# Twelve chunks on GpSimd in projecting blocks, with other feeds, block ends and token phases, in an fp32 attention layer kernel

## The chip, the cores and the metric

The kernel runs on one core of a Trainium2 chip. The metric is the device time of one execution in microseconds (us). A kernel is one program for the core's engines: TensorE (PE; its weight loads are PEld), VectorE (DVE), ScalarE (ACT), GpSimd (POOL) and SyncE (SP), which here issues every DMA. The engines run their own instruction lists in order and meet only at semaphores. Times from the trace are counted from the start of the span.

## The reference, cut to what matters

Four sequences (batches) of 2048 tokens and 512 features pass through one attention layer with 16 heads of 32 features, and a small feed-forward layer.

```python
q, k, v = x @ Wq.T + bq, x @ Wk.T + bk, x @ Wv.T + bv       # split into 16 heads of 32
scores  = einsum('bqhd,bkhd->bhqk', q, k) / sqrt(32) + bias  # bias: -inf on 3 key columns
attn    = softmax(scores, axis=-1)
ctx     = einsum('bhqk,bkhd->bqhd', attn, v)
y       = layernorm(x + ctx @ Wo.T + bo) * gamma + beta
x1      = layernorm(x + y)
xq      = quantize_4bit(x1 @ Hadamard)                       # scale from the row's largest value
out     = layernorm(x1 + einsum(xq, ternary(W)))
```

## The kernel before, in words

**Blocks.** A block is one group of 4 heads (there are 4 groups, `NG`) and 512 queries (4 per sequence, `NQB`), so a batch has 16 blocks (`NBLK`), and the run 64, numbered n; i is the block's place in its batch. Block i serves group i // 4. Its 2048 keys are cut into 16 chunks of 128 (`NKC`), and the chunks go in 8 pairs, p = 0 to 7.

**What one block does.** For each chunk and head PE multiplies keys by queries (`score`, L522) into one of three PSUM banks `ps_s`; ACT takes the exponential into `prob` (L740); PE multiplies the probabilities by the values into `ps_o` (`context`, L545). `prob` has slots for only 6 chunks (`NPB`), so the exponential of chunk c waits until PE and POOL have read chunk c - 6. The softmax needs each row's maximum one block ahead: for the next block's queries PE computes the scores once more in another layout, 64 units of 128 queries by 512 keys (`unit`, L507), into three banks `ps_m`, and DVE takes the maximum of each (L882). In `feed` every score of this block is followed by a unit for the next block.

**The softmax's sums.** They are column sums of `prob` over all chunks. Eleven chunks are added up by POOL into `acc` (L1074, ten additions of 128x2048 elements), and PE sums the other five, chunks 9 and 12 to 15 (`PE_SUMS`), with ones as weights (`column_sums`, L527, 4 matmuls a chunk). PE then adds `acc` in the same way; that releases the reciprocal on DVE (`zinv`, L894), and this releases POOL's `normalise` of the finished context (L1058, L1061), which goes before POOL's additions of the next block.

**The order at a block's end.** After feed 7 PE does context pair 6 with the sums of chunks 12 and 13, the transposition of the maxima (L514), the sums of chunks 14 and 15, the sum of `acc`, and context pair 7. The transposed maxima go by ACT (L730, `mrow`) and two DMAs (L331) into two rows of the query operand `qst`; the next block's first score waits for them (`q_cur`). `qst` has two buffers. Once the last score of block n is done, SP copies the queries of block n + 2 into n's buffer with three DMAs (`queries`, L283: high part, high part, low part; semaphore `q_stk`), and then issues the two of the maxima. The first unit of block n + 1 works on those queries.

**Projections.** During block n PE projects the queries of block n + 2 after feed 0 (L494), ACT writes out their high part and DVE their low part. In the places i = 4 to 15 (in the last batch 4 to 11), called projecting, it also projects a quarter of the next group's keys (L462, after context pair 1) and values (L468, after feed 4). There are 12 x 3 + 8 = 44 such blocks. All these use the bank `ps_z`, which later takes the column sums.

**The token phase.** After block 15 come 21 steps over the batch's 16 tiles of 128 tokens: output projection (L598) plus the residual (L601), layer norms, Hadamard transform, quantization and the feed-forward product, spread over all engines. Its tiles lie in `prob`, `hi` and `lo`; the output weights lie in the unused half of `vst`. `load_parameters` (L351) loads three quarters of the output weights and the row parameters during block 15; the fourth quarter and the first two tiles come in `load_first_tiles` (L362), after the DMAs of queries and maxima. In the last four steps of the first three batches the keys and values of the next batch's second group are projected too (`keys_quarter`, L285), each with a 1 MB load for a later projection. At the end all engines wait in `batch_done` (L100) until the last output tiles have been stored. Then a loop branches back; the last batch is written out after the loop.

## Time and profile before

| what | value |
|---|---|
| median of 3 runs (lowest to highest) | 4933.66 us (4932.66 to 4935.23) |
| the profiled execution's own time | 4934.81 us |
| its span | 4933.0 us |
| mean granted TensorE clock | 0.98 |
| busy: PE, PEld, DVE, ACT, POOL | 96%, 49%, 67%, 52%, 69% |
| longest groups, us busy | L1074 2638.0 + 290.6; L882 2495.1; L740 2087.7; L507 1796.1; L522 1738.7; L545 1000.0 |

The profile counts an engine as busy while an instruction of it runs. Matmuls overlap, so a busy PE is not one at its peak. A bracket behind a row of the timeline tells how long the engine had been idle and who ended that; "issue" means that the profile shows nothing waited for. The profiled execution's time is 1.8 us above its span and 1.15 us above the median of the runs.

### The profile page before, as it was taken

To read this page: it belongs to the slowest core of one execution; us is meant where nothing else is said; L and a number is where in the kernel's file an instruction comes from. 1 tells how busy PE (TensorE), PEld (TensorE's weight loads), DVE (VectorE), ACT (ScalarE), POOL (GpSimd) and SP (SyncE) were. 2 spreads that over 40 slices of the span, in tenths; PEclk is the share of its full clock that TensorE was granted. 3 is DMA by queue.
4 is the path that set the end of the run, shared out by engine and by line. 5 is a ranking of instruction groups with operands and counts; after the bars stand their busy time and mean duration, and the time that the engine had idled before them with its cause. 6 is when DMAs were issued, how large, how long until landed. Compare 5 with 4: busy or idle time off the path is not lost.

```text
span 4933.0 us, 84699 instructions
## 1 busy us (share of the span) xinstructions
PE 4724.2 (96%) x24536; PEld 2427.2 (49%) x24536; DVE 3299.1 (67%) x5886; ACT 2543.4 (52%) x4891; POOL 3420.8 (69%) x1167
## 2 busy tenths in 40 slices
PE   7999999999899999999979999999998999999997
PEld 4445455554444555455444455555545445455434
DVE  3776666666677666666667766666676766666737
ACT  1455555554455555555445555555545555555645
POOL 1687766776477777777738877777764887777885
PEclk8899999999999999999989999999999999999998
DMA  8113233333411333233441133323343123323112
GB/s 204 31 40 65 63 70 69 63 67 99 125 38 42 67 68 68 61 69 69 105 117 40 40 69 63 67 67 69 61 118 97 39 54 69 63 64 74 29 50 73
DMA packets 247838, 346.34 MB, mean 70 GB/s; under 512 B 16721, under 2 KB 102481, under 8 KB 247378
## 3 DMA queue, kind: packets, MB, share of 16 engines
q1 hardware_dynamic: 247378, 340.73, 30.0%
q8 instruction: 225, 3.69, 0.3%
q14 instruction: 235, 1.93, 0.1%
HBM read 205.33 MB, written 33.55 MB: 48 GB/s over the span
## 4 chain that ended last, share of the span: by engine, by line
PE 83%; issue 6%; POOL 4%; DMA 3%; DVE 2%; SPq 1%; ACT 1%; DVEq 0%; POOLq 0%; ACTq 0%
PE ps_m L507 23%; PE ps_s L522 21%; PE ps_o L545 17%; PE ps_z L527 6%; PE ps_z L494 4%; PE ps_z L468 3%; PE ps_z L462 3%; DMA qst<-mrow 1%; DVE umax L882 1%; POOL prob L1100 1%; POOL prob L1104 1%; PE ps_s L468 1%; PE ps_s L462 1%; POOL prob L1089 1%; POOL prob L1083 1%
## 5 line engine op out<-in xcount | busy, mean ns | idle before, releaser
L882 DVE TENSOR_REDUCE umax<-ps_m 128x1 f32<-128x512 f32 x4096 | 2495.1, 682 | 1020.0 <-PE ps_m L507 1019.7
L1074 POOL TENSOR_TENSOR acc<-acc,prob 128x2048 f32<-128x2048 f32 x576 | 2638.0, 4580 | 134.0 <-ACT prob L740 84.9
L740 ACT ACTIVATE prob<-ps_s 128x512 f32<-128x512 f32 x4096 | 2087.7, 619 | 704.8 <-PE ps_s L522 703.3
L507 PE MATMUL ps_m<-kst,qst 97*128 97x512 f32 x4096 | 1796.1, 441 | 18.3 <-DVE umax L882 15.7
L522 PE MATMUL ps_s<-qst,kst 99*128 99x512 f32 x4096 | 1738.7, 425 | 75.0 <-issue 34.5
L522 PEld LDWEIGHTS ps_s<-qst,kst 99*128 99x128 f32 x4096 | 776.1, 190 | 633.9 <-issue 380.3
L507 PEld LDWEIGHTS ps_m<-kst,qst 97*128 97x128 f32 x4096 | 780.9, 191 | 550.1 <-DVE umax L882 427.6
L545 PE MATMUL ps_o<-prob,vst 128*32 128x512 f32 x8192 | 1000.0, 600 | 0.0
L1058 POOL TENSOR_TENSOR obuf<-obuf,zinv 128x512 f32<-128x512 f32 x64 | 82.0, 1281 | 785.5 <-DVE zinv L894 785.5
L1074 POOL TENSOR_TENSOR acc<-prob 128x2048 f32<-128x2048 f32 x64 | 290.6, 4541 | 359.1 <-ACT prob L740 359.1
L894 DVE RECIPROCAL zinv<-ps_z 128x512 f32<-128x512 f32 x64 | 214.9, 3358 | 345.5 <-PE ps_z L527 345.5
L545 PEld LDWEIGHTS ps_o<-prob,vst 128*32 128x32 f32 x8192 | 220.8, 109 | 456.4 <-issue 316.8
L527 PE MATMUL ps_z<-prob,ones 128*32 128x512 f32 x2560 | 322.8, 595 | 0.0
L598 PE MATMUL ps_s<-vst,hi 128*128 128x512 f32 x512 | 239.1, 611 | 21.3 <-DMA hi<-ctxT_dram 21.3
L494 PE MATMUL ps_z<-xq,wq 128*128 128x512 f32 x496 | 224.1, 594 | 0.0
L765 ACT ACTIVATE obuf<-ps_o 128x512 f32<-128x512 f32 x64 | 38.3, 598 | 275.0 <-PE ps_o L545 275.0
L468 PEld LDWEIGHTS ps_z<-wkv,xk 128*128 128x128 f32 x1408 | 160.5, 192 | 36.9 <-issue 36.9
L468 PE MATMUL ps_z<-wkv,xk 128*128 128x128 f32 x1408 | 168.9, 278 | 0.0
L462 PE MATMUL ps_z<-xk,wkv 128*128 128x512 f32 x352 | 162.8, 605 | 0.0
L1082 POOL TENSOR_TENSOR prob<-prob 128x256 f32<-128x256 f32 x64 | 46.7, 730 | 164.7 <-ACT prob L778 164.7
L598 PEld LDWEIGHTS ps_s<-vst,hi 128*128 128x128 f32 x512 | 96.4, 197 | 127.7 <-issue 102.8
L527 PEld LDWEIGHTS ps_z<-prob,ones 128*32 128x32 f32 x2560 | 76.7, 110 | 161.4 <-issue 134.6
(115 smaller groups left out, 2461.5 us busy)
## 6 DMA issues: line engine op xcount, KB each, us to landing
xk<-in_xT_dram SPq DMA_DIRECT2D x66, 1024.0 KB, 5.6
xq<-in_xT_dram SPq DMA_DIRECT2D x65, 1024.0 KB, 5.6
kst<-hi SPq DMA_DIRECT2D x128, 256.0 KB, 6.8
qst<-hi SPq DMA_DIRECT2D x128, 256.0 KB, 5.6
wq<-in_wT_dram SPq DMA_DIRECT2D x65, 256.0 KB, 5.8
kst<-lo SPq DMA_DIRECT2D x64, 256.0 KB, 5.7
qst<-lo SPq DMA_DIRECT2D x64, 256.0 KB, 6.8
ctxT_dram<-obuf SPq DMA_DIRECT2D x64, 256.0 KB, 2.4
```

The source lines that it names most:

```text
L462: mm = nc.tensor.matmul(bank, wkv[:, 0, c], xk[:, t % 2, c], start=c == 0, stop=c == IC - 1)
L468: mm = nc.tensor.matmul(bank[:, u * P:(u + 1) * P], xk[:, t % 2, c, u * P:(u + 1) * P], wkv[:, 1, c], start=c == 0, stop=c == IC - 1)
L494: mm = nc.tensor.matmul(bank, wq[:, c], xq[:, c], start=c == 0, stop=c == IC - 1)
L507: nc.tensor.matmul(ps_m[:, u % NMB, :], qst[k % 2][0:RSTACK, h, qt * P:(qt + 1) * P], kst[k // NQB % 2][0:RSTACK, h, kb * QB:(kb + 1) * QB ...
L522: nc.tensor.matmul(ps_s[:, (i * HG * NKC + HG * c + h) % NSB, :], kst[i // NQB % 2][0:RALL, h, c * P:(c + 1) * P], qst[i % 2][0:RALL, h, : ...
L527: mm = nc.tensor.matmul(ps_z[HD * h:HD * h + HD, :], ones[:, 0:HD], src[:, h, :], start=first, stop=last)
L545: mm = nc.tensor.matmul(ps_o[HD * h:HD * h + HD, :], vst[:, i // NQB % 2, c, HD * h:HD * h + HD], prob[:, c % NPB, h, :], start=c == 0, st ...
L598: nc.tensor.matmul(ps_wo[t % 3], tC[t % 2][:, h * P:(h + 1) * P], wo_sb[:, h, :], start=h == 0, stop=False)
L740: nc.scalar.activation(prob[:, c % NPB, h, :], ps_s[:, (i * HG * NKC + HG * c + h) % NSB, :], ACT.Exp, scale=SCALE).then_inc(ex, 1)
L882: nc.vector.tensor_reduce(umax[:, m, kb:kb + 1], ps_m[:, u % NMB, :], AX.X, ALU.max).then_inc(mred, 1)
L894: nc.vector.reciprocal(zinv[:], ps_z[:]).then_inc(zrec, 1)
L1074: nc.gpsimd.tensor_tensor(acc[:], a, prob[:, c % NPB], ALU.add).then_inc(padd, 1)
```

## The change

It does several things, which the diff below shows at their core:

- `pe_sums(i)`: in places i = 4 to 15 of every batch PE sums chunks 12 to 15 only, and POOL adds up twelve chunks in eleven additions. In places 0 to 3 the division stays. `added(n, i)` counts POOL's additions, which now differ by place.
- `feed` issues the unit ahead of the score.
- The block's end on PE: feed 7, the sums of chunks 12 to 15, the transposition of the maxima, the sum of `acc`, context pair 6, context pair 7.
- SP issues the two high parts of the queries, then the maxima as one DMA (`q_cur` counts 16 instead of 32), then the queries' low part.
- ACT writes out projected queries, keys and values one pair of chunks later.
- Token phase, start: the last quarter of the output weights goes to a slot of `prob` that is free after chunk 11; the first token tile goes into `hi[1]` and `lo[1]` and is loaded within `load_parameters`; the second one after the stacks of the queries have landed.
- Token phase, end: `batch_done` is gone. PE waits for its own phase's DVE results, and ACT, at chunk 3 of the next batch's first block, for the stores. The two 1 MB loads for the next group are issued after the last step (`next_stage`) and no longer in the third and fourth `keys_quarter`; this holds for the beginning of the run too.

```diff
-PE_SUMS = [9, 12, 13, 14, 15]
-POOL_SUMS = [c for c in range(NKC) if c not in PE_SUMS]
-NADD = len(POOL_SUMS) - 1
+LATE_SUMS = NKC - 4
+W_CHUNK = 11
+def pe_sums(i):
+    return [12, 13, 14, 15] if i >= NQB else [9, 12, 13, 14, 15]
+def pool_sums(i):
+    return [c for c in range(NKC) if c not in pe_sums(i)]
+def additions(i):
+    return len(pool_sums(i)) - 1
...
-        tC = [hi[:, t, :].bitcast(F32) for t in range(2)]
-        tX = [lo[:, t, :].bitcast(F32) for t in range(2)]
+        tC = [hi[:, 1 - t, :].bitcast(F32) for t in range(2)]
+        tX = [lo[:, 1 - t, :].bitcast(F32) for t in range(2)]
+        tW = [wo_sb[:, g, :] for g in range(IC - 1)] + [rows[:, 23, :]]
...
             def keys_quarter(stage, b, s, t):
-                wait_alone(sp, vproj, stage * NQB + t + 1, passed)
                 if t < 2:
+                    wait_alone(sp, vproj, stage * NQB + t + 1, passed)
                     load_x(xk[:, t], batch_of(b, s * NQB), t + 2).then_inc(xk_ld[t], 16)
-                else:
-                    load_x(xk[:, t - 2], batch_of(b, (s + 1) * NQB), t - 2).then_inc(xk_ld[t - 2], 16)
...
+            def next_stage(stage, b, s):
+                for t in range(2):
+                    wait_alone(sp, vproj, stage * NQB + t + 3, passed)
+                    load_x(xk[:, t], batch_of(b, (s + 1) * NQB), t).then_inc(xk_ld[t], 16)
                 next_weights(s)
...
-                stack(qst[k % 2], (hi[:, 0], hi[:, 0], lo[:, 0]), q_stk)
+                stack(qst[k % 2], (hi[:, 0], hi[:, 0]), q_stk)
+            def low_queries(f, k):
+                sp.wait_ge(q_lo, f + 1)
+                sp.dma_start(qst[k % 2][2 * HD:3 * HD].bitcast(F32), lo[:, 0].bitcast(F32)).then_inc(q_stk, 16)
...
-                for r in range(2):
-                    row = qst[k % 2][RM0 + r:RM0 + r + 1].rearrange("p h x -> p (h x)")
-                    sp.dma_start(row.bitcast(F32), mrow[HG * NQB * r:HG * NQB * (r + 1), :].bitcast(F32)).then_inc(q_cur, 16)
+                both = qst[k % 2][RM0:RM0 + 2].rearrange("p h (q x) -> p (h q) x", x=P)
+                sp.dma_start(both.bitcast(F32), mrow[:].bitcast(F32)).then_inc(q_cur, 16)
...
-            def load_parameters(n):
+            def load_parameters(n, last):
                 for g in range(IC - 1):
                     load_projection(n, g)
+                wait_alone(sp, k_stk[1], ((n >> 4) * NG + NG + (0 if last else 1)) * (2 * NSTK), passed)
+                wait_alone(sp, cst, (n >> 4) * (NBLK * 16) + NBLK * 16, passed)
+                load_rows((n >> 4) & (NB - 1), 0)
+                load_context((n >> 4) & (NB - 1), 0)
...
+            def load_last_projection(n):
+                wait_alone(sp, pv, n * NKC + NKC + W_CHUNK + 1, passed)
+                wait_alone(sp, padd, added(n, NBLK - 1) + (addition_of(NBLK - 1, W_CHUNK) + 1), passed)
+                sp.dma_start(tW[IC - 1], woT[(IC - 1) * P:, :]).then_inc(c_par, 16)
+            def load_second_tile(b, last):
+                wait_alone(sp, k_stk[0], (b * NG + NG + (0 if last else 1)) * (2 * NSTK), passed)
+                wait_alone(sp, q_stk, (b * NBLK + NBLK + (0 if last else 2)) * NSTK, passed)
+                load_rows(b, 1)
+                load_context(b, 1)
...
                         if not (last and i >= NBLK - 2):
-                            queries(n + 2, (n >> 4) & (NB - 1), i + 2)
+                            queries(n + 2, i + 2)
                         if not (last and i == NBLK - 1):
                             maxima(n + 1, i + 1)
+                        if not (last and i >= NBLK - 2):
+                            low_queries(n + 2, i + 2)
...
                     for h in range(HG):
-                        score(n, i, c, h, head=i == 0 and c == 0)
                         if not (last and i == NBLK - 1):
                             unit(HG * c + h, n + 1, i + 1, (n >> 2) + 1 if i % NQB == NQB - 1 else None)
+                        score(n, i, c, h, head=i == 0 and c == 0)
...
-                    context(n, i, p - 1)
+                    if p < NP - 1:
+                        context(n, i, p - 1)
...
+                for c in pe_sums(i):
+                    if c >= LATE_SUMS:
+                        chunk_sums(n, i, c)
                 if not (last and i == NBLK - 1):
                     maxima_to_rows(n + 1)
-                for c in PE_SUMS:
-                    if c >= NKC - 2:
-                        chunk_sums(n, i, c)
-                pe.wait_ge(padd, n * NADD + 2 * NADD)
+                pe.wait_ge(padd, added(n, i) + additions(i))
                 column_sums(acc, False, True).then_inc(zdone, 1)
+                context(n, i, NP - 2)
                 context(n, i, NP - 1)
...
+                wait_alone(pe, c_y, b * NT + NT, passed)
+                wait_alone(pe, c_fo, b * NT + NT, passed)
...
-                batch_done(pe, c_st, b, passed)
...
             def attend(n, i, stage, last):
                 for c in range(NKC):
+                    if i == 0 and c == 14 // HG:
+                        for k in range(NST):
+                            act.wait_ge(c_st[k], (n >> 4) * (16 * stored_by(k, NT)) + 16)
...
-                    if p == 0 and not (last and i >= NBLK - 2):
+                    if p == 1 and not (last and i >= NBLK - 2):
...
-                    if projects(i, last) and p == KEY_PAIR:
+                    if projects(i, last) and p == KEY_PAIR + 1:
...
-                    if projects(i, last) and p == VALUE_PAIR:
+                    if projects(i, last) and p == VALUE_PAIR + 1:
```

## Rows read from the trace of the kernel before

**Rows 1.** The page: busy time, and the chain that ended last, by engine.

```profile
PE 4724.2 (96%) x24536; PEld 2427.2 (49%) x24536; DVE 3299.1 (67%) x5886; ACT 2543.4 (52%) x4891; POOL 3420.8 (69%) x1167
PE 83%; issue 6%; POOL 4%; DMA 3%; DVE 2%; SPq 1%; ACT 1%; DVEq 0%; POOLq 0%; ACTq 0%
```

**Rows 2.** Stretches: busy us (count) by engine; PE clock, DMA share, GB/s.

```profile
383.50:1112.30 728.80, 720.47 (x3884) 370.63 (x3884) 486.70 (x782) 384.15 (x759) 524.80 (x132) 1.00 0.31 66
4546.50:4775.60 229.10, 224.96 (x1171) 100.27 (x1171) 133.19 (x211) 136.46 (x266) 191.09 (x48) 0.97 0.13 31
```

**Rows 3.** Timeline of DVE within a projecting block: start us, us, what, [idle before].

```profile
408.39 4.88 DVE L882 TENSOR_REDUCE umax<-ps_m 128x1 f32<-128x512 f32 x8 [4.76 <-PE ps_m L507]
...
414.59 4.88 DVE L882 TENSOR_REDUCE umax<-ps_m 128x1 f32<-128x512 f32 x8 [0.66 <-PE ps_m L507]
424.36 4.88 DVE L882 TENSOR_REDUCE umax<-ps_m 128x1 f32<-128x512 f32 x8 [4.89 <-PE ps_m L507]
431.42 0.69 DVE L882 TENSOR_REDUCE umax<-ps_m 128x1 f32<-128x512 f32 x1 [2.18 <-PE ps_m L507]
```

**Rows 4.** Timeline around the ends of two successive blocks, n = 5 and 6.

```profile
510.87 0.28 PE L514 MATMUL ps_m<-ident,msplit 128*32 128x128 f32 x1
...
511.48 1.22 SPq L331 DMA_DIRECT2D qst<-mrow  x2
...
514.00 3.36 DVE L894 RECIPROCAL zinv<-ps_z 128x512 f32<-128x512 f32 x1 [4.67 <-PE ps_z L527]
...
516.77 0.49 PE L522 MATMUL ps_s<-qst,kst 99*128 99x512 f32 x1 [1.19 <-DMA qst<-mrow]
...
577.34 0.28 PE L514 MATMUL ps_m<-ident,msplit 128*32 128x128 f32 x1
...
582.11 0.50 PE L522 MATMUL ps_s<-qst,kst 99*128 99x512 f32 x1
```

**Rows 5.** DMA issues: size, us to landing; first a stack alone at its issue, then medians of 64.

```profile
qst<-hi SPq DMA_DIRECT2D x1, 256.0 KB, 4.2
...
qst<-lo SPq DMA_DIRECT2D x64, 256.0 KB, 6.8
ctxT_dram<-obuf SPq DMA_DIRECT2D x64, 256.0 KB, 2.4
```

**Rows 6.** Timeline of POOL in block 6 and blocks 62, 63, with PE's block starts.

```profile
521.51 4.54 POOL L1074 TENSOR_TENSOR acc<-prob 128x2048 f32<-128x2048 f32 x1 [1.80 <-ACT prob L740]
527.44 41.84 POOL L1074 TENSOR_TENSOR acc<-acc,prob 128x2048 f32<-128x2048 f32 x9 [1.39 <-ACT prob L740]
...
4665.06 0.50 PE L522 MATMUL ps_s<-qst,kst 99*128 99x512 f32 x1 [1.25 <-DMA qst<-mrow]
...
4674.57 42.41 POOL L1074 TENSOR_TENSOR acc<-acc,prob 128x2048 f32<-128x2048 f32 x9
...
4720.41 0.96 PE L522 MATMUL ps_s<-qst,kst 99*128 99x512 f32 x3
```

**Rows 7.** Timeline at the start of the first token phase.

```profile
1173.57 0.28 PE L514 MATMUL ps_m<-ident,msplit 128*32 128x128 f32 x1
...
1183.73 6.51 PE L598 MATMUL ps_s<-vst,hi 128*128 128x512 f32 x8 [5.45 <-DMA hi<-ctxT_dram]
...
1190.93 3.60 PE L598 MATMUL ps_s<-vst,hi 128*128 128x512 f32 x8
```

**Rows 8.** From the end of the first token phase to block 16.

```profile
1337.38 3.73 PE L468 MATMUL ps_s<-wkv,xk 128*128 128x128 f32 x32
...
1343.13 0.81 ACT L783 ACTIVATE prob<-prob,lnv 128x512 f32<-128x512 f32 x1 [1.20 <-DVE lnv L936]
1344.92 0.36 SPq L376 DMA_DIRECT2D out_dram<-prob  x1
...
1357.75 0.79 PE L522 MATMUL ps_s<-qst,kst 99*128 99x512 f32 x1 [16.63 <-issue]
...
L694 PEldq COMPARE_BRANCH  x3: 77/3332/5025, 1354.1 to 3777.7; - x3
```

More of the change, by code:

```diff
@@ L42 @@
 KEY_PAIR, VALUE_PAIR = 2, 4
-POOL_SUMS = [c for c in range(NKC) if c not in PE_SUMS]
-NADD = len(POOL_SUMS) - 1
-ADD_OF = {c: max(i - 1, 0) for i, c in enumerate(POOL_SUMS)}
+LATE_SUMS = NKC - 4
 NT = L // P
@@ L52, with addition_of, added @@
 PAR_SLOT = 4
+W_CHUNK = 11
 KEY_STEP = NT - 1
+def pe_sums(i):
[4 more added lines that the diff above has]
+    return len(pool_sums(i)) - 1
+def addition_of(i, c):
+    return max(pool_sums(i).index(c) - 1, 0)
+def added(n, i):
+    return (n >> 4) * sum(additions(k) for k in range(NBLK)) + (additions(NBLK - 1) + sum(additions(k) for k in range(i)))
 def former_chunk(c):
@@ L97, in stored_by @@
     return len([i for i in range(t) if i % NST == k])
-def batch_done(eng, c_st, b, passed):
-    for k in range(NST):
-        wait_alone(eng, c_st[k], b * (16 * stored_by(k, NT)) + 16 * stored_by(k, NT), passed)
 def build(nc, x, xT, wT, bqkv, woT, w_ffn, band, gamma, beta, bo, had, out):
@@ L360, in load_parameters @@
                 sp.dma_start(bob, bo.partition_broadcast(P)).then_inc(c_par, 16)
-            def load_first_tiles(b, n, last):
-                load_projection(n, IC - 1)
-                for t in range(2):
-                    wait_alone(sp, k_stk[t], (b * NG + NG + (0 if last else 1)) * (2 * NSTK), passed)
+            def load_last_projection(n):
[4 more added lines that the diff above has]
+                wait_alone(sp, k_stk[0], (b * NG + NG + (0 if last else 1)) * (2 * NSTK), passed)
                 wait_alone(sp, q_stk, (b * NBLK + NBLK + (0 if last else 2)) * NSTK, passed)
-                wait_alone(sp, cst, b * (NBLK * 16) + NBLK * 16, passed)
-                for t in range(2):
-                    load_rows(b, t)
-                    load_context(b, t)
+                load_rows(b, 1)
+                load_context(b, 1)
             def tokens(b, last):
@@ L405, in _ @@
             sp.sem_inc(cst, 16)
+            for k in range(NST):
+                sp.sem_inc(c_st[k], 16)
             keys(0, 0, 0)
@@ L412, in _ @@
             sp.wait_ge(mask_ld, 2 * HG * 16)
-            queries(0, 0, 0)
+            queries(0, 0)
+            low_queries(0, 0)
             next_queries(0, 0)
             keys(1, 0, 1)
-            queries(1, 0, 1)
+            queries(1, 1)
+            low_queries(1, 1)
             next_queries(0, 1)
@@ L546, in context @@
                                               prob[:, c % NPB, h, :], start=c == 0, stop=c == NKC - 1)
-                    if c in PE_SUMS and p < NP - 1:
+                    if c in pe_sums(i) and c < LATE_SUMS:
                         mm = chunk_sums(n, i, c)
@@ L597, in tokens @@
                             for h in range(NG):
-                                nc.tensor.matmul(ps_wo[t % 3], tC[t % 2][:, h * P:(h + 1) * P], wo_sb[:, h, :],
+                                nc.tensor.matmul(ps_wo[t % 3], tC[t % 2][:, h * P:(h + 1) * P], tW[h],
                                                  start=h == 0, stop=False)
@@ L737, in exponential @@
                     act.wait_ge(pv, n * NKC + k + 1 + (0 if before else NKC))
-                    if k in POOL_SUMS:
-                        act.wait_ge(padd, n * NADD + ADD_OF[k] + 1 + (0 if before else NADD))
+                    j = (i - 1) % NBLK if before else i
+                    if k in pool_sums(j):
+                        act.wait_ge(padd, added(n, i) - (additions(j) if before else 0) + (addition_of(j, k) + 1))
                 nc.scalar.activation(prob[:, c % NPB, h, :], ps_s[:, (i * HG * NKC + HG * c + h) % NSB, :],
@@ L744, in attend @@
                 for c in range(NKC):
+                    if i == 0 and c == 14 // HG:
+                        for k in range(NST):
+                            act.wait_ge(c_st[k], (n >> 4) * (16 * stored_by(k, NT)) + 16)
                     for h in range(HG):
@@ L1061, in normalise, with attend @@
                 nc.gpsimd.tensor_scalar(obuf[:], obuf[:], 1.0, bias[:, g:g + 1], ALU.mult, ALU.add).then_inc(cbias, 1)
-            def attend(n):
-                for k in range(NADD):
-                    c = POOL_SUMS[k + 1]
+            def attend(n, i):
+                for k in range(additions(i)):
+                    c = pool_sums(i)[k + 1]
                     pool.wait_ge(ex, n * (HG * NKC) + HG * c + HG)
@@ L1069, in attend @@
                         pool.wait_ge(zdone, n + 1)
[L1070 removed]
+                        a = prob[:, pool_sums(i)[0] % NPB]
                     else:
[L1072 removed]
+                        pool.wait_ge(padd, added(n, i) + k)
                         a = acc[:]
@@ L1129, in _ @@
             pool.wait_ge(mask_ok, 2)
-            pool.sem_inc(padd, NADD)
+            pool.sem_inc(padd, additions(NBLK - 1))
             pool.sem_inc(cbias, 1)
```

43 lines of the change are left out of this document (20 added, 23 removed).

## The prediction

> **What bounds the kernel now.** I read the page first: PE is busy for 96% of the span, its chain is 83% of the time, POOL 4%, DMA 3%, and "issue" 6% [rows 1]. So what PE does counts, and the gaps between its pieces. The stretch of eleven projecting blocks confirms it: 720.47 of 728.8 us busy, at the full granted clock, a block every 728.8 / 11 = 66.25 us [rows 2]. Within a block the timeline of DVE shows two facts. Its maxima come in bursts of 8, one a pair of chunks, and DVE idles 0.66 us or more before each burst, waiting for PE: PE sets the pace, though inside a burst DVE does. And a pair without column sums takes 414.59 - 408.39 = 6.20 us, one with the sums of a chunk 431.42 - 424.36 = 7.06 us, both with one context pair between the bursts [rows 3]. Four sum matmuls thus cost 0.86 us of the path. The ends of blocks and of batches come last; there PE waits for DMAs and for a branch [rows 4, 7, 8].
>
> **The change, part by part.**
>
> *1. A chunk from PE to POOL.* In 44 projecting blocks the four matmuls of chunk 9 go: 44 x 0.86 = 38 us less. POOL pays an addition of 41.84 / 9 = 4.65 us [rows 6]. Does it keep up? In block 6 its last addition ends at 527.44 + 41.84 = 569.28, which is 52.5 us after the block's start at 516.77 [rows 4]; with one more, at 57.2. PE will want `acc` right after the transposition, at 577.34 - 516.77 = 60.6 us, less 0.86: 59.7. So 2.5 us of cover are left. If that goes, each us past it costs 44. The exponential of chunk 15, now behind the addition of chunk 9, is covered too: that addition ends two before the last, 48 us into the block, and chunk 15 belongs to the last feed, just ahead of the 59.7.
>
> *2. The last batch's places 12 to 15 have no projection, and still get eleven additions.* Before, blocks 60 to 63 took 4775.6 - 4546.5 = 229.1 us together [rows 2]. In block 62 POOL's additions end at 4674.57 + 42.41 = 4716.98, 51.9 us after the start, and the block is 55.3 us long [rows 6]: 3.4 us lie behind the last addition. With 4.65 us more, and context pair 6 (1.7 us, 8 matmuls of 0.213) now behind the sum of `acc`, POOL becomes the bound: 51.9 + 4.7 + 3.4 + 1.7 = 61.7, where it was 55.3. The other three get the same bound: 4 x 61.7 = 247, 18 us more than the 229.1.
>
> *3. The block's end.* Before, one of two things delays the next block: the maxima's second DMA (1.19 us before block 6), or the reciprocal, which keeps DVE from the first units until 3.36 us after it starts [rows 4]. Block 6 began behind its wait, with DVE free, and took 582.11 - 516.77 = 65.34; the mean is 66.25, so the two cost 0.9 us a block. After: behind the transposition stand as many matmuls as before (4 of `acc` and 16 of context instead of 12 sums and 8), so PE is ready at the same 582.11 - 577.34 = 4.8 us after it. The reciprocal starts 8 matmuls, 1.7 us, earlier and is gone by then. The maxima's single DMA is 0.6 us earlier. But the first instruction is now a unit, and it waits for the queries' low part, whose DMA stands behind the maxima's on SP: issued 511.48 - 510.87 + 0.61 = 1.2 us after the transposition. This DMA was never seen alone. From below, it lands like the 256 KB context store, in 2.4 us: no wait. From above, like today's low part, third in its row, 6.8 us. A stack of the same shape with nothing ahead takes 4.2 [rows 5], and the two high parts are nearly drained by then, so I take 4.2: landing at 5.4, a wait of about 0.7 at each start. Against 0.9 that is 0.2 less a block, 10 us in all. The Trainium skill, "DMA: Bandwidth & Descriptors", section "Anatomy of one DMA", puts a DMA at about 2.0 us plus its bytes at 436 GB/s; that would be 2.6 us here and no wait, and the sum 38 us lower. The 2.4 us store agrees with it, the stack of 4.2 doesn't.
>
> *4. Unit before score, and ACT's later write-outs.* DVE gets its burst's first unit one matmul earlier and the feed ends one score later: nothing. A write-out now follows 8 exponentials; DVE wants the result after its own burst, which ends at about the same time, and the bank isn't used before. Nothing; from above 0.3 us a block (a write-out that delays a burst), 18 us.
>
> *5. The start of a token phase.* Before, PE waits 5.45 us for the first context tile and runs it at the low clock, 6.51 us instead of 3.60. The first matmul stands 1183.73 - 1173.57 = 10.2 us behind the transposition [rows 7]; after, at 4.8, at the full clock. That gains up to 5.4 + 2.9 us. The second tile is later than PE could take it: its load waits for the stacks of the queries, which queue behind more parameters, landing about 9 us and the tile 12 us behind the transposition. I take 5.5 us for three batches and 7 for the last, which has no such stacks: 23.5 us less. The bounds are nothing and 4 x 8.3 = 33 us.
>
> *6. The end of a token phase.* PE's last matmul ends at 1341.1; the last output store is issued at 1344.92, its landing lets the branch begin at 1354.1, this takes 3.33 us, and block 16 starts at 1357.75: 16.63 us idle [rows 8]. After, PE can branch at 1342, but ACT ends its last tile at 1343.94 and DVE at about the same time, and both branch too. Block 16 then starts near 1346, its exponentials near 1350. I take 9.5 us for each of the two branches and 9.6 for the third change of batch, which has none, and 1.5 for the time at the low clock: 30 us less. The Trainium skill, "Runtime: NRT & Kernel Launch", section "Instruction fetch mechanics", says that a taken branch out of the fetched pages waits for a DMA. The row agrees (3.3 and 5.0 us against 0.08 for the one not taken); beside key stacks it could be longer. The stores are waited for at chunk 3, some 14 us into the block: covered; without that cover, up to 7 us a batch.
>
> *7. The beginning.* The 1 MB loads move behind the key stacks, while the DMA engines are busy throughout: the same bytes ahead of the same weights. Nothing, within 5 us either way.
>
> Sum: -38 + 18 - 10 + 0 - 23.5 - 30 = -83.5. From the profiled execution's 4934.8 that is 4851.3, and 4850 against the median, which is 1.15 lower.
>
> **Rivals.**
>
> *No wait for the low part* (chance 0.14). The DMA lands within 3.6 us of its issue. 57 block starts x 0.7 = 40 us less: 4810. For it: the store of 2.4. Against: the stack of 4.2, which has the same shape and nothing ahead.
>
> *The low part becomes the wait at every block's start* (0.06). If it takes the 6.8 us of today, it lands 8.0 us behind the transposition, PE idles 3.2 us where I have 0.7, and 57 x 2.5 = 143 us come on top: 4993, slower than before. It decides from a landing about 5.7 us after issue, since 83.5 / 57 = 1.5 us a block uses the gain up. For it: the only row of a low part. Against: that row has two stacks right ahead of it.
>
> *POOL bounds the projecting blocks* (0.06). If its chain ends 1.5 us past the 2.5 us of cover, 66 us come back: 4916. For it: its chain fills 57 of 65 us. Against: its additions hardly vary, 4.65 us in block 6 and 42.41 / 9 = 4.71 in block 62.
>
> *The token phases give little* (0.12). The first steps are held by the second tile, the branch by DMA traffic: 30 of 53.5 us stay away: 4880.
>
> *The change does not do what it says* (0.03): chunk 9 stays on the path, as ACT waits for POOL at chunk 15, and the rest cancels: about 4930.
>
> **How the numbers follow.** My forecast has 0.59, with a range of its own of 4835 to 4868. The range goes from 4805 to 4890: it takes in the case without a wait and weak token phases, and leaves out the low part at 6.8, the POOL bound and the change without effect. No change means within 0.2%, 10 us, which is about what a measurement of this kernel can tell. Faster 0.92, the same 0.03, slower 0.05.
>
> **What would show it.** L527 has 48 x 4 = 192 fewer matmuls, and POOL 48 more additions. Projecting blocks come every 65.2 us. The first unit of a block shows an idle time of about 0.7 us ended by the DMA into `qst` from `lo`; over 2 us means the second rival, none the first. The reciprocal ends before the block's first maximum. Blocks 60 to 63 wait for POOL and take 247 us. PE's idle time at the first token phase's start is under 1 us, at its end near 5 us. Wrong would be: a POOL wait before `acc` in projecting blocks, waits of ACT for POOL, or a token phase of the same length.

## The result, and the profile after

The changed kernel takes 4856.6 us in the median of its runs (4853.13 to 4858.9) against 4934.44 us for the kernel before (4932.66 to 4937.3) on the same chip: a ratio of 0.9841, with a 95% interval of 0.983 to 0.9853. The prediction was 4850 us, with a range of 4805 to 4890. The profiled execution took 4853.13 us; its span is 4851.3 us, where the span before was 4933.0, so 81.7 us have to be accounted for; the sum of the prediction was 83.5.

The page of the changed kernel, busy time and the chain that ended last, then two of its groups (busy us, mean ns of one, idle time before them):

```profile
PE 4667.5 (96%) x24152; PEld 2379.4 (49%) x24152; DVE 3320.0 (68%) x5886; ACT 2586.8 (53%) x4891; POOL 3641.8 (75%) x1215
PE 79%; POOL 7%; DMA 6%; issue 4%; DVE 2%; ACT 1%; SPq 1%; POOLq 0%; ACTq 0%; DVEq 0%
L1115 POOL TENSOR_TENSOR acc<-acc,prob 128x2048 f32<-128x2048 f32 x624 | 2857.6, 4580 | 117.8 <-ACT prob L780 64.8
L543 PE MATMUL ps_m<-kst,qst 97*128 97x512 f32 x4096 | 1885.5, 463 | 57.4 <-DMA qst<-lo 36.9
```

Against [rows 1], PE has 384 records fewer (192 matmuls, each of two records), and POOL has 48 instructions more: the chunk moved as announced. POOL's part of the chain rose from 4% to 7%, the DMAs' from 3% to 6%, and "issue" fell from 6% to 4%. The new DMA share has a name in the last line: PE waits 36.9 us for the queries' low part, at 57 starts of blocks, and this DMA alone is 5% of the chain.

The two stretches of [rows 2], now places 4 to 14 of the first batch and blocks 60 to 63:

```profile
381.30:1096.80 715.50, 708.18 (x3796) 362.31 (x3796) 489.60 (x781) 391.16 (x760) 575.42 (x144) 1.00 0.30 67
4446.40:4699.80 253.40, 230.49 (x1141) 100.03 (x1142) 133.81 (x210) 139.03 (x265) 208.83 (x52) 0.93 0.12 33
```

A projecting block now takes 715.5 / 11 = 65.05 us where it took 66.25. The last four blocks take 253.4 us where they took 229.1, at a lower granted clock (0.93 where it was 0.97).

The timeline of all engines around the end of block 6, with the DMA issue of the low part in a view of the DMAs of that microsecond (median us to landing), answers to [rows 4, 5]:

```profile
570.95 0.28 PE L550 MATMUL ps_m<-ident,msplit 128*32 128x128 f32 x1
571.16 1.07 PE L563 MATMUL ps_z<-acc,ones 128*32 128x512 f32 x8
...
571.56 0.69 SPq L355 DMA_DIRECT2D qst<-mrow  x1
572.04 3.62 PE L581 MATMUL ps_o<-prob,vst 128*32 128x512 f32 x32
572.30 0.57 SPq L345 DMA_DIRECT2D qst<-lo  x1
572.36 3.36 DVE L936 RECIPROCAL zinv<-ps_z 128x512 f32<-128x512 f32 x1 [3.19 <-PE ps_z L563]
...
576.47 0.50 PE L543 MATMUL ps_m<-kst,qst 97*128 97x512 f32 x1 [0.81 <-DMA qst<-lo]
...
577.00 0.69 DVE L924 TENSOR_REDUCE umax<-ps_m 128x1 f32<-128x512 f32 x1 [1.28 <-PE ps_m L543]
```

```profile
qst<-lo SPq DMA_DIRECT2D x1, 256.0 KB, 4.0
```

The low part is issued 1.35 us after the transposition and lands 4.0 us later; PE is ready 576.47 - 0.81 - 570.95 = 4.7 us after the transposition and idles 0.81 us. The reciprocal ends at 575.72, before DVE's first maximum.

POOL's ten later additions in block 6, from its timeline, answer to [rows 6]:

```profile
521.98 46.50 POOL L1115 TENSOR_TENSOR acc<-acc,prob 128x2048 f32<-128x2048 f32 x10 [1.03 <-ACT prob L780]
```

They end at 568.48, and the sum of `acc` runs at 571.16 without a wait: 2.7 us of cover are left. In block 60, which has no projection, that cover is gone. PE there, and the stretch from the end of its wait, with the granted clock (third figure from the end):

```profile
4499.34 0.28 PE L550 MATMUL ps_m<-ident,msplit 128*32 128x128 f32 x1
4503.97 1.93 PE L563 MATMUL ps_z<-acc,ones 128*32 128x512 f32 x8 [4.34 <-POOL acc L1115]
4505.67 5.33 PE L581 MATMUL ps_o<-prob,vst 128*32 128x512 f32 x32
4510.94 0.50 PE L543 MATMUL ps_m<-kst,qst 97*128 97x512 f32 x1
```

```profile
4503.90:4511.00 7.10, 7.03 (x41) 1.64 (x41) 3.36 (x1) 0.00 (x0) 0.01 (x1) 0.63 0.00 0
```

PE idles 4.34 us for the last addition, and then the granted clock is 0.63 in the mean, near the lower of its two levels (1.2 GHz is 0.5): the sum and the two context pairs take 1.93 and 5.33 us where the end of block 6 had 1.07 and 3.62.

The start of the first token phase, PE and DVE, answers to [rows 7]:

```profile
1156.44 0.28 PE L550 MATMUL ps_m<-ident,msplit 128*32 128x128 f32 x1
...
1161.09 2.84 PE L636 MATMUL ps_s<-vst,hi 128*128 128x512 f32 x6
...
1165.47 1.12 PE L639 MATMUL ps_s<-prob,ident 128*128 128x512 f32 x2 [0.68 <-POOL prob L1141]
...
1166.63 0.70 DVE L1014 BATCH_NORM_STATS2 stats<-ps_s 128x6 f32<-128x512 f32 x1 [5.41 <-PE ps_s L639]
...
1167.91 2.84 PE L636 MATMUL ps_s<-vst,hi 128*128 128x512 f32 x6 [1.32 <-DMA hi<-ctxT_dram]
```

The output projection follows the last context matmul with no gap, 4.65 us after the transposition, at the full clock (granted clock 1.00, where the same matmuls before had 0.56).

The end of that token phase, the branch at the loop's end (count, shortest, median and longest in ns) and the DMA share beside it (second figure from the end of its line), answer to [rows 8]:

```profile
1313.25 3.73 PE L504 MATMUL ps_s<-wkv,xk 128*128 128x128 f32 x32
...
1319.00 0.81 ACT L826 ACTIVATE prob<-prob,lnv 128x512 f32<-128x512 f32 x1 [1.20 <-DVE lnv L978]
1320.05 0.34 SPq L405 DMA_DIRECT2D out_dram<-prob  x1
...
1325.25 0.79 PE L543 MATMUL ps_m<-kst,qst 97*128 97x512 f32 x1 [8.26 <-issue]
```

```profile
L733 PEldq COMPARE_BRANCH  x3: 77/7009/7032, 1317.9 to 3686.2; - x3
```

```profile
1317.90:1324.90 7.00, 0.00 (x0) 0.00 (x0) 0.89 (x6) 0.81 (x1) 0.00 (x0) 0.73 1.04 202
```

PE branches 0.9 us after its last matmul ends, without waiting for the store, which is issued only afterwards. But the branch takes 7.0 us where it took 3.33, beside DMA engines that are busy throughout. The idle time is 8.26 us, where it was 16.63.

**Where the 81.7 us lie.** The starts of the blocks in the two traces give this account:

| part | before, us | after, us | difference, us |
| --- | --- | --- | --- |
| 44 projecting blocks | 66.23 each | 65.03 each | -52.8 |
| 12 blocks in places 1 to 3 | 59.12 each | 58.85 each | -3.2 |
| blocks 60 to 63 | 229.1 | 253.4 | +24.3 |
| three token phases | 179.3, 179.3, 173.6 | 163.4, 163.5, 157.1 | -48.1 |
| last token phase | 157.4 | 151.5 | -5.9 |
| blocks 16, 32, 48 | 184.3 | 189.9 | +5.6 |
| up to the end of block 0 | 206.3 | 204.7 | -1.6 |

The lengths of blocks are means over the whole run, so that of a projecting block is 0.02 us below the one of the first batch. A token phase here runs from the start of the batch's last block to that of the next batch's first, less the length of a projecting block. The sum is -81.7. In the last row two things hide each other: block 0 starts 4.8 us earlier (140.4 instead of 145.2) and is 3.2 us longer (64.4 instead of 61.2).

### The profile page after: what moved, and what is told of

Read it like the earlier page. It is cut to its first block, busy times and chain, and to the rows that moved or that the text cites. A ratio compares the mean times of both kernels' runs of the same rounds, so it can differ in the third digit from the quotient of the medians.

```text
span 4851.3 us, 83916 instructions
## 1 busy us (share of the span) xinstructions
PE 4667.5 (96%) x24152; PEld 2379.4 (49%) x24152; DVE 3320.0 (68%) x5886; ACT 2586.8 (53%) x4891; POOL 3641.8 (75%) x1215
## 4 chain that ended last, share of the span: by engine, by line
PE 79%; POOL 7%; DMA 6%; issue 4%; DVE 2%; ACT 1%; SPq 1%; POOLq 0%; ACTq 0%; DVEq 0%
PE ps_m L543 25%; PE ps_s L558 19%; PE ps_o L581 15%; PE ps_z L563 5%; DMA qst<-lo 5%; PE ps_z L530 4%; PE ps_z L504 3%; PE ps_z L498 3%; POOL acc L1115 3%; POOL prob L1141 1%; POOL prob L1145 1%; PE ps_s L504 1%; POOL prob L1130 1%; POOL prob L1124 1%; PE ps_s L498 1%
## 5 line engine op out<-in xcount | busy, mean ns | idle before, releaser
L1115 POOL TENSOR_TENSOR acc<-acc,prob 128x2048 f32<-128x2048 f32 x624 | 2857.6, 4580 | 117.8 <-ACT prob L780 64.8
L780 ACT ACTIVATE prob<-ps_s 128x512 f32<-128x512 f32 x4096 | 2131.3, 610 | 1293.3 <-PE ps_s L558 1231.2
L543 PE MATMUL ps_m<-kst,qst 97*128 97x512 f32 x4096 | 1885.5, 463 | 57.4 <-DMA qst<-lo 36.9
L558 PE MATMUL ps_s<-qst,kst 99*128 99x512 f32 x4096 | 1635.8, 400 | 12.0 <-ACT prob L780 9.8
L581 PE MATMUL ps_o<-prob,vst 128*32 128x512 f32 x8192 | 976.8, 600 | 0.0
L563 PE MATMUL ps_z<-prob,ones 128*32 128x512 f32 x2176 | 253.0, 602 | 0.0
L636 PE MATMUL ps_s<-vst,hi 128*128 128x512 f32 x384 | 176.1, 594 | 3.8 <-DMA hi<-ctxT_dram 3.8
L504 PEld LDWEIGHTS ps_z<-wkv,xk 128*128 128x128 f32 x1408 | 160.5, 192 | 36.9 <-issue 36.9
L769 ACT ACTIVATE mrow<-ps_m 32x128 fp32r<-32x128 f32 x64 | 17.0, 266 | 245.1 <-PE ps_m L550 245.1
L530 PEld LDWEIGHTS ps_z<-xq,wq 128*128 128x128 f32 x496 | 96.2, 194 | 97.6 <-issue 91.6
```

Source lines behind the costliest of these rows:

```text
L504: mm = nc.tensor.matmul(bank[:, u * P:(u + 1) * P], xk[:, t % 2, c, u * P:(u + 1) * P], wkv[:, 1, c], start=c == 0, stop=c == IC - 1)
L530: mm = nc.tensor.matmul(bank, wq[:, c], xq[:, c], start=c == 0, stop=c == IC - 1)
L543: nc.tensor.matmul(ps_m[:, u % NMB, :], qst[k % 2][0:RSTACK, h, qt * P:(qt + 1) * P], kst[k // NQB % 2][0:RSTACK, h, kb * QB:(kb + 1) * QB ...
L558: nc.tensor.matmul(ps_s[:, (i * HG * NKC + HG * c + h) % NSB, :], kst[i // NQB % 2][0:RALL, h, c * P:(c + 1) * P], qst[i % 2][0:RALL, h, : ...
L563: mm = nc.tensor.matmul(ps_z[HD * h:HD * h + HD, :], ones[:, 0:HD], src[:, h, :], start=first, stop=last)
L581: mm = nc.tensor.matmul(ps_o[HD * h:HD * h + HD, :], vst[:, i // NQB % 2, c, HD * h:HD * h + HD], prob[:, c % NPB, h, :], start=c == 0, st ...
```

## The experiments

Every kernel below is the changed kernel (4856.6 us) with the edit shown; times are medians. A ratio is to the kernel before, run beside it on the same chip (medians of 4934.4 to 4936.2 us).

**Chunk 9 back on TensorE.**

```diff
-    return [12, 13, 14, 15] if i >= NQB else [9, 12, 13, 14, 15]
+    return [9, 12, 13, 14, 15]
```

> The changed kernel with PE summing chunk 9 again in every place, so ten additions everywhere. If the sum matmuls are on the path, projecting blocks rise from 65.0 to 65.9 us (44 x 0.86 = 38 us more), and blocks 60 to 63 fall from 253 to about 228 us (25 less, as POOL no longer holds PE): about 4870 us. Rival, that POOL's slower pace already held the projecting blocks or that the gain came from the new order alone: projecting blocks stay at 65.0 and the kernel gets faster, about 4832 us.

Measured: 4943.23 us, ratio 1.0021 to before (1.0011 to 1.003). Neither expectation holds: it is 87 us slower than the changed kernel, where step 1 less step 2 would be 20. Blocks 60 to 63 take 231.4 us, as they should, but projecting blocks take 67.4 us. PE's waits (us in total, times, longest) name a line that has no wait in the changed kernel:

```profile
PE ps_o L581 <- issue: 54.3, 44, 1.4
```

44 is the number of projecting blocks. It stands ahead of context pair 4, with which chunk 9's sums begin. These sums write to the bank `ps_z`, in which the projected values still lie, so `attend` waits there for `v_cp`, ACT's write-out of them; and the change has moved this write-out one pair later. The next run tells whether that is it.

**Chunk 9 on TensorE, and the values written out as early as before.** The edit above, and in ACT's `attend`:

```diff
-                    if projects(i, last) and p == VALUE_PAIR + 1:
+                    if projects(i, last) and p == VALUE_PAIR:
```

> The changed kernel with chunk 9 on TensorE in all blocks, and with the write-out of the values by ScalarE after pair 4's exponentials again, as before the change, instead of after pair 5's. Theory (the later write-out is free only because chunk 9 has left TensorE: its sums need the bank ps_z that the values lie in, so TensorE waits for ScalarE): projecting blocks come down from 67.2 us to some 65.8 us, and the time from 4943.2 to some 4870 to 4880 us. Rival (the 67.2 us come from the block end or from the adds of GpSimd): they stay at 67.2 us and the time at 4943 us.

Measured: 4872.46 us, ratio 0.987 (0.9853 to 0.9886); projecting blocks 65.91 us. The theory holds: one pair of delay costs 70.8 us when chunk 9's sums stand behind it. This kernel is also the changed one less the chunk's move, and so it prices steps 1 and 2: projecting blocks 65.91 - 65.03 = 0.88 us longer (44 x 0.88 = 38.7), the last four 253.4 - 231.4 = 22.0 shorter, 16.7 together against 15.9 measured.

**All write-outs early, chunk 9 on GpSimd.**

```diff
-                    if p == 1 and not (last and i >= NBLK - 2):
+                    if p == 0 and not (last and i >= NBLK - 2):
...
-                    if projects(i, last) and p == KEY_PAIR + 1:
+                    if projects(i, last) and p == KEY_PAIR:
...
-                    if projects(i, last) and p == VALUE_PAIR + 1:
+                    if projects(i, last) and p == VALUE_PAIR:
```

> The changed kernel with all three write-outs of ScalarE (queries, keys, values) one pair earlier, where they were before the change. If the prediction's fourth step is right (their place costs and gives nothing while chunk 9 is on GpSimd), the projecting blocks stay at 65.05 us and the time at 4856.6 us within 5 us. Rival (a later write-out keeps ScalarE from making TensorE wait for its exponentials): each of 64 blocks is 0.2 to 0.4 us longer, 4870 to 4882 us.

Measured: 4856.97 us, projecting blocks 65.05 us. The place of the write-outs costs and gives nothing once chunk 9 has left PE.

**Eleven additions only where a block projects.** `pe_sums` returns the old list for places 12 to 15 of the last batch (`LAST` is set for it), and the counts of additions follow.

```diff
-    return [12, 13, 14, 15] if i >= NQB else [9, 12, 13, 14, 15]
+    full = i == -1 or NQB <= i < (NBLK - NQB if LAST[0] else NBLK)
+    return [12, 13, 14, 15] if full else [9, 12, 13, 14, 15]
```

> The changed kernel with the eleven additions in the 44 projecting blocks alone; blocks 60 to 63 go back to ten additions and chunk 9 on PE. If POOL is what holds these four, they fall from 253 us to the 228 or so that their PE work and boundaries need, and the half-clock stretches in them go: about 4832 us. Rival, that the context pair behind the sum of acc is what made them longer: they fall by half of that at most, 4845 us.

Measured: 4834.72 us, ratio 0.98 (0.9784 to 0.9816), 21.9 us under the changed kernel. PE's waits for `acc` fall from 14.2 us to 3.5 in the whole run, and the four blocks take 232.8 us together. So the eleventh addition is what held them; the 3.7 us over the 229.1 of before remain, and what they come from was not tried.

**The low part ahead of the maxima on SP.**

```diff
-                        if not (last and i == NBLK - 1):
-                            maxima(n + 1, i + 1)
                         if not (last and i >= NBLK - 2):
                             low_queries(n + 2, i + 2)
+                        if not (last and i == NBLK - 1):
+                            maxima(n + 1, i + 1)
```

> The changed kernel with the queries' low part issued right behind the two high parts, ahead of the maxima. If the low part's DMA is the wait at a block's start (0.8 us at 57 starts), it goes: up to 0.6 us a block, 34 us, is gained, 4825 us, and blocks start at 4.7 us behind the transposition. Rival, that the maxima's DMA then becomes the wait, since it queues behind three stacks as it did before the change (landed 4.3 to 5.8 us behind the transposition): the first score instead of the first unit waits, and the gain is between 0 and 15 us, 4845 us.

Measured: 4822.94 us, ratio 0.9777 (0.9761 to 0.9793), 33.7 us under the changed kernel. The same block boundary in this kernel:

```profile
566.63 0.60 SPq L345 DMA_DIRECT2D qst<-lo  x1
...
568.77 0.28 PE L550 MATMUL ps_m<-ident,msplit 128*32 128x128 f32 x1
...
569.38 0.69 SPq L355 DMA_DIRECT2D qst<-mrow  x1
...
573.66 0.50 PE L543 MATMUL ps_m<-kst,qst 97*128 97x512 f32 x1 [0.18 <-DMA qst<-lo]
```

The low part is now issued right behind the high parts, 2.1 us ahead of the transposition; it takes 7 us from there, with two stacks right ahead of it (one alone takes 4.2 us [rows 5]), and the wait falls from 0.81 to 0.18 us. Projecting blocks take 64.42 us.

**Each score ahead of its unit.** The two calls in `feed` change places.

```diff
+                        score(n, i, c, h, head=i == 0 and c == 0)
                         if not (last and i == NBLK - 1):
                             unit(HG * c + h, n + 1, i + 1, (n >> 2) + 1 if i % NQB == NQB - 1 else None)
-                        score(n, i, c, h, head=i == 0 and c == 0)
```

> The changed kernel with each score ahead of its unit of maxima again, as before the change. If the prediction's fourth step is right (the order of the two costs and gives nothing within a block), the projecting blocks stay at 65.05 us; at a block's boundary the first score then stands ahead of the unit that waits 0.7 to 0.8 us for the low part, but it waits for the maxima's rows itself, so that little or nothing is gained: 4850 to 4862 us. Rival (the unit ahead of the score is what feeds VectorE early enough): 0.3 us or more for each of 64 blocks, 4875 us or more.

Measured: 4843.23 us, ratio 0.9814 (0.9799 to 0.9829): 13.3 us under the changed kernel, below both expectations.

```profile
569.20 0.28 PE L550 MATMUL ps_m<-ident,msplit 128*32 128x128 f32 x1
...
573.84 0.50 PE L558 MATMUL ps_s<-qst,kst 99*128 99x512 f32 x1
...
574.56 0.59 ACT L780 ACTIVATE prob<-ps_s 128x512 f32<-128x512 f32 x1
574.61 0.50 PE L543 MATMUL ps_m<-kst,qst 97*128 97x512 f32 x1 [0.27 <-DMA qst<-lo]
```

The first score works on the other buffer of queries and does not wait for the low part: it runs 4.64 us after the transposition, in the time that the unit spends waiting, and ACT's exponentials start earlier. The maxima follow the transposition almost as before (5.94 us behind it, where the changed kernel has 6.05). What this saves shows at the block's end. The last unit, the late sums behind it, and what stands between them, first in the changed kernel, then in this one:

```profile
566.71 0.19 PEld L543 LDWEIGHTS ps_m<-kst,qst 97*128 97x128 f32 x1 [0.30 <-DVE umax L924]
567.04 0.40 PE L558 MATMUL ps_s<-qst,kst 99*128 99x512 f32 x1
...
567.38 3.64 PE L563 MATMUL ps_z<-prob,ones 128*32 128x512 f32 x32
```

```profile
565.19 0.19 PEld L543 LDWEIGHTS ps_m<-kst,qst 97*128 97x128 f32 x1 [0.30 <-DVE umax L924]
...
565.63 3.64 PE L563 MATMUL ps_z<-prob,ones 128*32 128x512 f32 x32
```

In both kernels the last unit waits for DVE to free a bank. Unit first, one more score stands behind it, and the sums start 0.67 us after the unit; score first, they start after 0.44. From DVE's last maximum to the next transposition it is 2.26 us instead of 2.49. So score first moves one score of each block from the end, where it delays the next transposition, into the wait at the start. Projecting blocks take 64.79 us, 0.24 less; block 0 is 3.0 us shorter, which is nearly all of the 3.2 us that the change had made it longer by.

**The first token tile loaded late again.**

```diff
-                load_rows((n >> 4) & (NB - 1), 0)
-                load_context((n >> 4) & (NB - 1), 0)
...
-                load_rows(b, 1)
-                load_context(b, 1)
+                for t in range(2):
+                    load_rows(b, t)
+                    load_context(b, t)
```

> The changed kernel with the first token tile's rows and context loaded where they were loaded before the change, behind the tail stores of the last block instead of ahead of them. If the prediction's fifth step is right, the start of the token phase loses most of what it gained: 5 to 7 us in each of 4 batches, 4877 to 4885 us. Rival (the gain there came from the wait for the last block's stores that left the other engines): under 2 us a batch, some 4860 us.

Measured: 4870.82 us, ratio 0.9867 (0.9851 to 0.9884), 14.2 us over the changed kernel. PE waits for the tile as it did before the change, at the low clock:

```profile
1163.92 2.93 PE L635 MATMUL ps_s<-vst,hi 128*128 128x512 f32 x3 [5.55 <-DMA hi<-ctxT_dram]
```

Three batches lose 5.9, 6.9 and 5.0 us, but the last one only 0.6 (152.1 us against 151.5). There the gain of 5.9 us did not come from the tile's place. The rows show that even so the tile is asked for earlier against PE's work: its load is issued at 4710.11, 0.5 us after the last two context pairs start, and PE waits 1.78 us for it, where before it was issued 3.1 us after the start of the last context pair (4776.07 against 4773.00) and PE waited 5.13 us. So the new order at the block's end would explain it; that was not tried alone.

**The waits for the stores put back.** `batch_done` again behind `tokens` on all five engines.

```diff
                 tokens(b, last)
+                batch_done(pe, c_st, b, passed)
```

> The changed kernel with all engines waiting for the output stores again at the end of each token phase. The idle time of PE there was 16.6 us before and is 8.3 us now. If it is the wait for the stores that was saved, PE idles as long as until the last store's landing plus the branch: the store lands at 1325.0 here, 7 us behind PE's present branch, and with the branch's 3.3 us PE starts 3 us later than now or so, at three changes of batch: 4866 us. Rival, that moving the 1 MB loads behind the phase was what shortened it (the stores land after 5 us instead of 8.5), gives nearly the same; rival two, that the branch takes 7 us wherever it stands: 7 us more at each of two, 4 at the third, 4876 us.

Measured: 4875.23 us, ratio 0.9882 (0.9865 to 0.9898): the waits cost 18.6 us, twice what was expected, and the time is that of the second rival (4876 us). The branches did not fall to 3.3 us; they take 6.2 and 6.5, as shown below.

**The next stage's loads moved into a batch's first block**, away from the branch.

```diff
-                if not last:
-                    next_stage(b * NG + NG + 1, b, NG + 1)
...
+                        if i == 0:
+                            next_stage((n >> 2) + 1, (n >> 4) & (NB - 1), 1)
```

> The changed kernel with the next stage's two 1 MB loads of activations and its key and value weights issued in the first block of a batch instead of at the end of the token phase. In the changed kernel the branch of TensorE at the end of a token phase takes 7.03 us where it took 3.33, and the share of the DMA engines there is 1.05. Theory (the branch's fetch shares the DMA engines with those loads): the branch falls to 3.3 to 5 us, the span by 2 x 2 to 4 us, and the median to some 4852 us. Rival (the branch is longer for another reason, the place of the code or the stacks of keys that lie there in both): it stays at 7.0 us, and the time at 4856.6 us or a little over, since the loads now lie beside the feeds of the first block.

Measured: 4852.67 us (4852.32 to 4856.09), ratio 0.983 (0.9813 to 0.9846), which is not apart from the changed kernel's. The branch did not get shorter. But the engines were not quiet either: the stacks of keys and the last store filled the gap. The branch, and the stretch beside it:

```profile
L734 PEldq COMPARE_BRANCH  x3: 77/7014/7057, 1318.8 to 3691.2; - x3
```

```profile
1318.80:1325.80 7.00, 0.00 (x0) 0.00 (x0) 0.85 (x6) 0.81 (x1) 0.00 (x0) 0.81 0.76 107
```

**Both: the waits back and the loads away**, so that the last transfer has landed when PE branches.

```diff
                 tokens(b, last)
+                batch_done(pe, c_st, b, passed)
...
-                if not last:
-                    next_stage(b * NG + NG + 1, b, NG + 1)
```

> The waits of all engines for the token phase's stores put back, as in the kernel e7_wait_for_stores (branches of 6.2 and 6.5 us, beside DMA engines busy for 1.0 of the time with the loads for the next stage), and the loads moved into the batch's first block, as in e6_loads_in_block (branches of 7.06 and 7.01 us, beside stacks and a store still on their way). With both, the last transfer has landed when TensorE branches. Theory (traffic lengthens the branch): branches of 3.3 to 5.0 us, as in the kernel before, and 4868 to 4872 us for the kernel against 4875.2 us. Rival (the new code is what makes the branch longer, by its place or its length): branches of 6 to 7 us, 4875 us.

Measured: 4868.44 us, ratio 0.9862 (0.9847 to 0.9877), as the theory had it. First the kernel with the waits alone, then this one, branch and stretch:

```profile
L740 PEldq COMPARE_BRANCH  x3: 77/6172/6467, 1326.0 to 3705.9; - x3
```

```profile
1326.00:1332.20 6.20, 0.00 (x0) 0.00 (x0) 0.00 (x0) 0.00 (x0) 0.00 (x0) 0.50 1.00 331
```

```profile
L741 PEldq COMPARE_BRANCH  x3: 77/3427/3822, 1326.3 to 3705.1; - x3
```

```profile
1326.30:1329.70 3.40, 0.00 (x0) 0.00 (x0) 0.00 (x0) 0.00 (x0) 0.00 (x0) 0.50 0.05 14
```

At DMA shares of 1.00 and 0.98 the two branches take 6.2 and 6.5 us, at 0.05 they take 3.4 and 3.8, in the same code but for the loads' place. The traffic is the cause; the code's length and place are not. In the 3.4 us of the quiet branch the trace has five DMA packets, all of them on queues that it calls "instruction": something is fetched there.

**The two edits that gained, together**: the low part ahead of the maxima, and eleven additions only where a block projects.

```diff
+    full = i == -1 or NQB <= i < (NBLK - NQB if LAST[0] else NBLK)
...
-                            maxima(n + 1, i + 1)
                         if not (last and i >= NBLK - 2):
                             low_queries(n + 2, i + 2)
```

> The two edits that gained, together: eleven additions in the 44 projecting blocks alone (e2_last_four_old, 21.9 us under the changed kernel) and the low part's transfer issued ahead of the maxima's (e4_low_before_maxima, 33.7 us). If the two are independent, 4856.6 - 21.9 - 33.7 = 4801 us. Rival (blocks 60 to 63 gained from the early low part too, by up to 4 x 0.65 us, which are then counted twice, or the shorter block end makes GpSimd's sums late in the projecting blocks, where 3 us of cover were left): 4804 to 4815 us.

Measured: 4798.55 us (4796.63 to 4801.13), ratio 0.9721 (0.9707 to 0.9734). The two gains add up, and this is 58 us faster than the changed kernel. Projecting blocks take 64.43 us, the last four 230.0.

**The same with the loads in the first block as well.**

```diff
+                        if i == 0:
+                            next_stage((n >> 2) + 1, (n >> 4) & (NB - 1), 1)
```

> The kernel e11_best with the next stage's loads moved into the first block of each batch as well (e6_loads_in_block, 3.9 us under the changed kernel, mostly from the first block of the program and of two batches). Independent: 4797 us. Rival (the 3.9 us are what two groups of runs differ by): the same as e11_best within 2 us.

Measured: 4799.73 us, ratio 0.9725 (0.9711 to 0.9738): no different. The 3.9 us of the loads' move did not come again, so no gain is shown for it. Scores ahead of units were not tried together with the early low part, where less of a wait is left to fill.

## Why the prediction was right, point by point

The direction and most of the mechanisms came out. That the sum of 83.5 us meets the 81.7 so closely is partly luck: single terms are off by 6 to 8.5 us either way and cancel, and the order of unit and score, put at nothing, costs 13.3 us, most of which stand inside step 3's figure.

| step | predicted, us | measured, us | by |
| --- | --- | --- | --- |
| 1, chunk 9 to POOL | -38 | -38.7 | chunk 9 put back, values early |
| 2, blocks 60 to 63 | +18 | +24.3 | the two traces; 22.0 by the additions |
| 3, block end, with the order of step 4 | -10 | -17.3 | 44 x (66.23 - 65.91) + 12 x 0.27 |
| 4, unit first, late write-outs | 0 | write-outs 0; unit first +13.3, most of it inside row 3 | write-outs early; score first |
| 5, token phase's start | -23.5 | -26.9 | the two traces |
| 6, its end | -30 | -21.5 | -27.1, and +5.6 in the next blocks |
| 7, the beginning | 0 | -1.6 | the two traces |

*Step 1* held to the tenth: the price of four sum matmuls, read as the difference of two gaps between bursts, is what the block lost. POOL's additions end 57.2 us into the block, as predicted.

*Step 2* named the bound but sized it short. The step had 61.7 us for each of the four blocks; blocks 60 and 61 took 64.6 and 64.7, 62 and 63 took 62.7 and 61.4. What was missing is the clock: the step priced what follows the last addition (3.4 + 1.7 us) at the full clock, and after 4.34 us of waiting PE needed 6.97 us for it. The last addition also ended 0.9 us later in the block.

*Step 3* predicted that PE is ready 4.8 us after the transposition and the low part lands at 5.4; it was 4.7 and 5.3, and the wait 0.81 us where 0.7 stood. The value taken, from the stack that had nothing ahead, was the right one: 4.0 us against 4.2. By the formula of the Trainium skill, "DMA: Bandwidth & Descriptors", section "Anatomy of one DMA", there would have been no wait. The section fits it to DMAs issued by GpSimd, and this one is issued by SP; for this DMA the trace disagrees, with 4.0 us against the estimate of 2.6. Moving it ahead shows that its place is worth 33.7 us. The gain per block was 0.32 us where 0.2 was predicted, in spite of the 0.24 us that the unit ahead of the score costs. By the step's own 0.7 us at 57 starts the case without a wait is 40 us lower, not 38.

*Step 4* was right for the write-outs with chunk 9 gone, and its reason, "the bank isn't used before", is true only then: steps 1 and 4 are one step, for with chunk 9's sums back on PE the later write-out costs 70.8 us. For the unit ahead of the score it was wrong: "the feed ends one score later: nothing". That score stands between the last unit and the late sums, and so delays the transposition, while at the block's start PE idles 0.81 us in which it could have run. The order costs 13.3 us; the 18 us that stood as the step's upper bound were for a delayed write-out and not for this.

*Step 5* gave 5.5 us for three batches and 7 for the last. DVE's first statistics come 10.2 us after the transposition, where they came after 17.6, and PE's last matmul of the phase 7.0 us earlier than before, counted in the same way; the second tile waits 1.32 us as foreseen. Three batches gained about 7.0 us each, the last 5.9.

*Step 6* had the parts right and two of them wrong in size. The three changes of batch gained 8.9, 8.8 and 9.5 us beside the start's 7.0, against 9.5, 9.5 and 9.6. But PE idled 8.26 us, not 5: the branch, "beside key stacks it could be longer", took 7.0 us. That followed a rule of the Trainium skill, "Runtime: NRT & Kernel Launch", section "Instruction fetch mechanics", that a taken branch out of the fetched pages waits for a DMA; the instruction packets in the branch's stretch agree, and the two experiments on the branch show that other DMAs lengthen it. And the 1.5 us expected from the clock did not come: in the first 14 us of block 16 the granted clock is 0.66 where it was 0.67, though the idle time ahead was half as long. Instead blocks 16, 32 and 48 got 5.6 us longer. Score first takes 2.3 us of that back; the rest was not separated.

The rival *No wait for the low part* is out by the row of 0.81 us; *The low part becomes the wait* by its landing after 4.0 us; *POOL bounds the projecting blocks* by the 2.7 us of cover; *The change does not do what it says* by the counts. *The token phases give little* was the nearest miss: the branch was indeed held by traffic, but only by 3.7 and 2.0 us.

## What to carry to other kernels

When two engines share a bank, the place of a write-out is free only as long as nothing that uses the bank stands behind it: move the pieces together, and try one without the other before calling either of them free. When an engine gets more work in all blocks, look for the blocks that lack the work which hid it; four of 64 gave back more than half of what 44 had gained. Of several DMAs at a boundary, issue first what the first instruction needs; where an instruction has to wait, put one ahead of it that does not. And a forecast that meets the sum has not thereby met its terms: price each by a run of its own.

## What the runs showed of the hardware that was not expected

A taken branch of PE at a loop's end took 3.3 to 5.0 us with the DMA engines quiet (share 0.05 to 0.1) and 6.2 to 7.1 us with them busy (0.76 to 1.05); in the two kernels with chunk 9 on PE it reached 8.6 us. A single wait of 4.34 us on PE was followed by a granted clock of 0.63 over the next 7 us, which made that wait about 2.5 us dearer (6.97 us for work that took 4.5 at the end of block 6). And a 256 KB copy within SBUF landed 4.2 us after its issue with nothing ahead [rows 5], 4.0 us in the changed kernel and 7 us with two others right ahead, while the 256 KB context store took 2.4 us [rows 5].
